# A Mamba-2 block with a mixture of experts behind it: other turns, engines and loads for the weights of the projection's first group

## The reference, cut to what matters

```
h = rmsnorm(hidden_states, ln1_w)              # 2048 x 512
zxbcdt = h @ in_proj_w                         # 512 x 2576
z, xb, Bc, Cc, dt = split(zxbcdt)              # 1024, 256, 256, 1024, 16 columns
xBC = silu(causal_depthwise_conv([xb, Bc, Cc]))  # 4 taps
dt = softplus(dt + dt_bias)                    # step sizes
y = ssd_chunked(...) ; y = rmsnorm(y * silu(z)) @ out_proj_w
```

## Time and profile before

| | |
|---|---|
| time, median of 3 runs | 1441.54 us |
| the profiled execution, its time | 1440.74 us |
| its span | 1439.0 us |
| mean granted clock of PE | 0.986 |
| PE busy | 1379.0 us (96%) |
| DVE busy | 956.3 us (66%) |
| ACT busy | 640.9 us (45%) |
| POOL busy | 479.8 us (33%) |
| PE's first matmul of the projection | at 16.92 us |
| first matmul of groups 1, 2, 3 | at 89.31, 154.65, 219.61 us |
| last instructions of PE in the projection | 28 short matmuls from 279.69 us |

### The profile page before, as it was taken

One profiled execution on the slowest core, in us unless ns is written; L12 is line 12 of the kernel. 1 busy time (PEld: TensorE's weight loads), 2 busy tenths in 40 slices (PEclk: granted clock), 3 DMA queues, 4 the chain that ended last, 5 costly groups with the idle time before them and its releaser, 6 DMA issues.

```text
span 1439.0 us, 20651 instructions
## 1 busy us (share of the span) xinstructions
PE 1379.0 (96%) x7252; PEld 1107.2 (77%) x7252; DVE 956.3 (66%) x1314; ACT 640.9 (45%) x1123; POOL 479.8 (33%) x455
## 2 busy tenths in 40 slices
PE   6899999989999998999999999999999889999998
PEld 4677777756666665788888888888887689999997
DVE  6879697789999997233333333333336779999997
ACT  4444454455555554311121112121111348888886
POOL 2612021247777775210101101011101027556563
PEclk9999999999999999999999999999999979999999
DMA  9122221833333221500001000002033933444331
GB/s 206 60 106 103 84 89 59 245 107 108 117 118 114 103 104 52 191 30 15 30 15 29 29 15 29 15 29 95 0 110 126 340 99 66 80 73 76 72 48 22
DMA packets 84359, 122.62 MB, mean 85 GB/s; under 512 B 28591, under 2 KB 44975, under 8 KB 84272
## 3 DMA queue, kind: packets, MB, share of 16 engines
q1 hardware_dynamic: 71488, 103.62, 21.9%
q0 software_dynamic: 8736, 16.79, 6.7%
q10 hardware_dynamic: 4048, 1.10, 0.3%
HBM read 81.37 MB, written 43.78 MB: 87 GB/s over the span
## 4 chain that ended last, share of the span: by engine, by line
PE 56%; DVE 2%; issue 1%; ACT 0%; DMA 0%; POOL 0%; DVEq 0%; ACTq 0%; POOLq 0%
PE fin_bank L1894 53%; PE fin_bank L2035 1%; PE fin_bank L2054 1%; DVE onehot L1803 0%; PE fin_bank L1962 0%; DMA xs<-xn_rows,idx 0%; PE fin_bank L1950 0%; DVE ff_w_lo L1695 0%; ACT gu_hi L1586 0%; DVE fi_bn L1730 0%; DVE gu_lo L1824 0%; ACT ff_w_hi L1564 0%; PE fin_bank L2027 0%; POOL out_dram L1518 0%; PE fin_bank L1960 0%
## 5 line engine op out<-in xcount | busy, mean ns | idle before, releaser
L1657 DVE TENSOR_TENSOR ff_prod<-ff_prod,fin_bank 128x512 f32<-128x512 f32 x64 | 44.0, 688 | 263.1 <-PE fin_bank L1894 263.1
L1894 PE MATMUL fin_bank<-ff_hT_hi,ff_w_hi 128*128 128x512 f32 x512 | 202.7, 396 | 3.2 <-DVE ff_w_lo L1665 3.2
L1894 PE MATMUL fin_bank<-ff_hT_hi,ff_w_lo 128*128 128x512 f32 x512 | 202.4, 395 | 0.0
L1894 PE MATMUL fin_bank<-ff_hT_lo,ff_w_hi 128*128 128x512 f32 x512 | 202.4, 395 | 0.0
L1448 POOL TENSOR_TENSOR ff_w_lo<-ff_stage,ff_w_hi 128x1024 fp32r<-128x1024 f32 (+1 forms) x24 | 56.5, 2355 | 411.1 <-ACT ff_w_hi L1554 406.3
L543 DVE SCALAR_TENSOR_TENSOR conv_acc<-raw,conv_w,conv_acc 128x512 f32<-128x512 f32 x144 | 115.7, 804 | 41.6 <-ACT raw L349 35.4
L648 PE MATMUL pj_bank<-hT_hi,w_in_hi 128*128 128x512 f32 x336 | 136.0, 405 | 6.5 <-POOL w_in_lo L296 4.0
L1539 ACT ACTIVATE ff_prod<-fin_bank 128x512 f32<-128x512 f32 x64 | 38.3, 598 | 231.5 <-PE fin_bank L1894 231.5
L648 PE MATMUL pj_bank<-hT_lo,w_in_hi 128*128 128x512 f32 x336 | 133.7, 398 | 0.0
L648 PE MATMUL pj_bank<-hT_hi,w_in_lo 128*128 128x512 f32 x336 | 132.8, 395 | 0.0
L1824 DVE TENSOR_TENSOR gu_lo<-wx,gu_hi 128x1408 fp32r<-128x1408 f32 (+1 forms) x79 | 124.9, 1620 | 1.8 <-ACT gu_hi L1586 1.8
(11 more groups left out here) (287 smaller groups left out, 3213.3 us busy)
## 6 DMA issues: line engine op xcount, KB each, us to landing
cv_rows<-cst SPq DMA_DIRECT2D x12, 1024.0 KB, 4.3
cv<-cv_rows SPq DMA_DIRECT2D x16, 768.0 KB, 4.3
zs_rows<-zst SPq DMA_DIRECT2D x8, 1024.0 KB, 6.5
zs<-zs_rows SPq DMA_DIRECT2D x16, 512.0 KB, 5.3
wx<-in_L_ffn_Wg_dram SPq DMA_DIRECT2D x8, 704.0 KB, 8.6
wx<-in_L_ffn_Wu_dram SPq DMA_DIRECT2D x8, 704.0 KB, 8.5
w_raw<-in_L_attn_in_proj_w_dram SPq DMA_DIRECT2D x32, 128.0 KB, 3.6
x<-_attn_hidden_states_dram SPq DMA_DIRECT2D x16, 256.0 KB, 5.4
```

Source lines behind the costliest of these rows:

```text
L1657: eng.tensor_tensor(prod[c][:, :], prod[c][:, :], up_ps[c][:, :], ALU.mult).then_inc(s["prod"], 1)
L1894: mm = eng.matmul(ps, w[a], x[b], start=first and i == 0, stop=last and i == 2)
```

## The change

1. **Order in group 0.** `first_products(0)` was dt, ch 0-6, then z and ch in turn, then z 5-7. It is now dt, ch 0-4, then z and ch in turn (z 0 at place 6, ch 8 at place 13, z 4 at place 14), then z 7.
2. **Loads.** C and z are no longer loaded in pairs of heads but as they lie in DRAM, by three DMAs: C's first half, all of z, C's second half. They go to places of their own (`c_raw`, `z_raw`), laid over buffers that are needed later (`zst`, `cst[1]`, `hT_hi1` and `hT_lo1`), and the pairing is done by the access pattern with which ACT and DVE read them (`by_pair`, `pairs`). The twelve small vectors are issued by SP, between C's first half and z.
3. **Low parts.** All by DVE. In ACT's and DVE's list the quarters follow each other as C, z, C, z ("czcz"). ACT makes two high parts at each of places 2 to 7; DVE makes two low parts at each of the places in the table `LOWS`.
4. **Turned rows.** `turned` stands at the start of places 16 to 19 on ACT and DVE, ahead of the work on that place's block.
5. **Step sizes.** For groups 1 to 3 the dt block uses weights `wdt` of 32 columns, 16 of high and 16 of low parts side by side: 8 matmuls. The two halves land in different partitions, are turned together, and DVE adds them (one more instruction of 128 x 64 in `dt_first`). `wdt` is filled by two small copies of DVE ahead of `made`.

```diff
     if g == 0:
-        order = [("dt", 0)] + conv[0:7]
-        rest = conv[7:12]
-        for i in range(5):
-            order += [z[i], rest[i]]
-        return order + z[5:8]
+        order = [("dt", 0)] + conv[0:5]
+        for i in range(7):
+            order += [z[i], conv[5 + i]]
+        return order + z[7:8]
...
+        LOWS = {2: KD, 3: KD + 2, 6: 2 * KD, 8: 2 * KD + 2, 10: 3 * KD, 12: 3 * KD + 2}
...
+        def by_pair(t, kk, a):
+
+            return t[:, kk, a * DI // 2:(a + 1) * DI // 2].rearrange("p (b j n) -> p j b n", b=2, j=HPG)
+
+        def pairs(t, kk, at):
+            return t[:, kk, at:at + DI // 2].rearrange("p (j b n) -> p j b n", j=HPG, b=2)
...
-            for a, (dst, src) in heads_raw(W_C, c0):
-                eng.dma_start(dst, src).then_inc(s[f"wc{a}_dma"], 16)
-            for a, (dst, src) in heads_raw(W_Z, 0):
-                eng.dma_start(dst, src).then_inc(s["wz_dma"], 16)
+            half = DI // 2
+            eng.dma_start(c_raw[0][:, :, :], wr[:, :, c0:c0 + half]).then_inc(s["wc0_dma"], 16)
+            small_vectors(eng)
+            eng.dma_start(z_raw[:, :, :], wr[:, :, 0:DI]).then_inc(s["wz_dma"], 16)
+            eng.dma_start(c_raw[1][:, :, :], wr[:, :, c0 + half:c0 + DI]).then_inc(s["wc1_dma"], 16)
```

POOL's part goes:

```diff
-                    if g == 0 and 4 <= n <= 7:
-                        for j in range(2):
-                            split_z((n - 4) // 2, 2 * (n - 4) % KD + j)
```

In the loops over the places, `turned` moves on ACT (and in the same way on DVE) from behind the place's work to ahead of it:

```diff
                 for n, (kind, i) in enumerate(ORDER[g]):
+                    if g + 1 < NGRP and AT_TURN <= n < AT_TURN + KD:
+                        turned(g + 1, n - AT_TURN)
                     if kind == "dt":
...
-                    if g + 1 < NGRP and AT_TURN <= n < AT_TURN + KD:
-                        turned(g + 1, n - AT_TURN)
```

DVE's low parts:

```diff
-                    if g == 0 and 1 <= n <= KD:
-                        split(2 * KD + n, n - 1, W_C + 512, W_C + 1024)
+                    if g == 0 and n in LOWS:
+                        for j in range(2):
+                            split_heads(LOWS[n] + j)
...
+            def split_heads(i):
+
+                kk, kind, a = i % KD, "czcz"[i // KD], i // (2 * KD)
+                eng.wait_ge(s["w_hi"], KD + i + 1)
+                at = (W_C if kind == "c" else W_Z) + a * 512
+                src = by_pair(c_raw[a], kk, 0) if kind == "c" else by_pair(z_raw, kk, a)
+                eng.tensor_tensor(pairs(w_lo, kk, at), src, pairs(w_hi, kk, at).bitcast(F32), ALU.subtract)\
+                   .then_inc(s["wx_lo" if kind == "c" else "wz_lo"], 1)
```

The dt block of groups 1 to 3 on PE, in `product`:

```diff
+                if g and kind == "dt":
+                    eng.wait_ge(s["made"], 1)
+                    for k in range(KD):
+                        if k < KD - 1:
+                            eng.matmul(ps[0:2 * HEADS, :], wdt[:, k, :], x[0][:, k, :], start=(k == 0), stop=False)
+                        eng.matmul(ps[0:HEADS, :], wdt[:, k, 0:HEADS], x[1][:, k, :], start=False, stop=False,
+                                   skip_group_check=True)
+                    eng.matmul(ps[0:2 * HEADS, :], wdt[:, KD - 1, :], x[0][:, KD - 1, :], start=False, stop=True)\
+                       .then_inc(s["block_ps"], 1)
+                    return
```

More of the change, by code:

```diff
@@ L96, in project @@
         lnq = [sb(f"lnq{i}", [P, 4, UPG]) for i in range(2)]
+        with nc.sbuf_tensor("z_raw", [P, KD, DI], F32) as z_raw:
+            pass
         hT_hi = [keep["hT0"][0], sb("hT_hi1", [P, KD, GR], F32R)]
@@ L103, in project @@
         ztnh = [sb(f"ztnh{i}", [P, GR]) for i in range(2)]
-        cst = [sb(f"cst{i}", [P, UPG, 4, P]) for i in range(2)]
+        cst = [sb("cst0", [P, UPG, 4, P])]
+        with nc.sbuf_tensor("c_raw1", [P, KD, DI // 2], F32) as c_raw1:
+            pass
+        cst.append(sb("cst1", [P, UPG, 4, P]))
+        with nc.sbuf_tensor("c_raw0", [P, KD, DI // 2], F32) as c_raw0:
+            pass
+        c_raw = [c_raw0, c_raw1]
         zst = [sb(f"zst{i}", [P, UPG, 4, P]) for i in range(2)]
-        dtT = sb("dtT", [HEADS, GR])
+        dtT = sb("dtT", [2 * HEADS, GR])
+        wdt = sb("wdt", [P, KD, 2 * HEADS], F32R)
         sp = sb("sp", [P, 7, UPG * HEADS])
@@ L162, in xin_ready, with small_vectors @@
             return (s[f"xin_dma{u}"], 16) if g == 0 else (xin_next[g % 2], 16 * (1 + g // 2))
-        def heads_raw(at, src):
-            for a in range(2):
-                for b in range(2):
-                    for k in range(KD):
-                        cols = slice(at + a * DI // 2, at + (a + 1) * DI // 2)
-                        yield a, (w_raw[:, k, cols].rearrange("p (j b n) -> p j b n", j=HPG, b=2)[:, :, b, :],
-                                  wr[:, k, src + (2 * a + b) * HPG * DST:src + (2 * a + b + 1) * HPG * DST]
-                                  .rearrange("p (j n) -> p j n", j=HPG))
+        def by_pair(t, kk, a):
+            return t[:, kk, a * DI // 2:(a + 1) * DI // 2].rearrange("p (b j n) -> p j b n", b=2, j=HPG)
+        def pairs(t, kk, at):
+            return t[:, kk, at:at + DI // 2].rearrange("p (j b n) -> p j b n", j=HPG, b=2)
+        def small_vectors(eng):
+            cw, cb = ins["L0_attn_conv_w"], ins["L0_attn_conv_b"]
+            nb = 2 * DXB // P
+            with nc.allow_non_contiguous_dma("small vectors"):
+                loads = [(a_neg[:, :], ins["L0_attn_A_log"].partition_broadcast(P)),
+                         (dt_bias[:, :], ins["L0_attn_dt_bias"].partition_broadcast(P)),
+                         (conv_w[:, 0:nb, :], cw[0:2 * DXB, :].rearrange("(k p) t -> p k t", p=P)),
+                         (conv_b[:, 0:nb], cb[0:2 * DXB].rearrange("(k p) -> p k", p=P))]
+                for a in range(2):
+                    for b in range(2):
+                        half, at, src = slice(b * HD, (b + 1) * HD), nb + HPG * a, 2 * DXB + (2 * a + b) * HPG * DST
+                        loads += [(conv_w[half, at:at + HPG, :],
+                                   cw[src:src + HPG * DST, :].rearrange("(j n) t -> n j t", j=HPG)),
+                                  (conv_b[half, at:at + HPG],
+                                   cb[src:src + HPG * DST].rearrange("(j n) -> n j", j=HPG))]
+                for dst, src in loads:
+                    eng.dma_start(dst, src).then_inc(s["v_dma"], 16)
         @block.sync
@@ L549, in silu_ch @@
                 eng.wait_ge(s["ch_tanh"], m + 1)
+                if ch % 4 == 0 and q == 1:
+                    eng.wait_ge(s["wx_lo"], 3 * KD)
                 if ch % 4 == 0 and q >= 2:
@@ L576, in _ @@
             for k in range(KD):
[L577 removed]
+                split_heads(k)
             def tables():
```

83 lines of the change are left out of this document (38 added, 45 removed).

## The result

The changed kernel takes 1430.72 us (median of 4 runs, 1429.10 to 1431.76), the kernel before 1440.84 us beside it (1439.84 to 1441.88): a ratio of 0.993, 95% interval 0.9918 to 0.9941. The forecast was 1432.0 in a range of 1428 to 1437.

A forecast was written before the change was run, and what follows sets the result against it. The prediction took PE's waits in the projection, with DVE behind them, as the bound. Gains of 3.4 + 2.8 + 1.9 + 1.2 = 9.3 us took 1440.74 to 1431.4, for a median 1432 us; range 1428 to 1437.

The forecast's parts named there:

- Group 0: Projection's first group: group 1 begins at 85.9 instead of 89.31 us, a gain of 3.4 us.
- The list of DVE: DVE's summed work in group 0 up to place 12, which z 4 waits for; it ends at 62.96 us.
- the wait for POOL's halo: Group 0, place 8: DVE waits 1.35 us for POOL's halo copy, which stands behind `norms`, before ch 6's taps.
- in front of z 4: Group 0, place 14: PE stands 5.0 us for DVE's low parts of place 12; the wait has moved, not gone.
- The low clock's cost: Group 0, behind PE's pause at z 4: a clock loss of 1.5 us, bounds 0 and 2.
- Step sizes: dt blocks of groups 1 to 3: 12 to 8 matmuls at 0.232 us each, a gain of 2.8 us.
- The change from 1 to 2: Group 2 begins at 152.7 instead of 154.65 us after a 1.5 us wait for the last turned part; gain 1.9.
- the one from 2 to 3: Group 3 begins at 218.35 instead of 219.61 us, with PE still standing 0.85 us for a turned part; gain 1.2.
- The start: Loads and first rows ahead of the projection: counted as 0, with bounds of 2 us later and 1 us earlier.
- z's load being late: Rival at the start: z lands after 29 us and holds ACT before ch 2's copy; 1434 to 1437 us, 12%.
- The rule of ring order: Start: one queue's descriptors go in order, so small vectors land behind C's first half, not before about 17.6 us.
- DVE keeps up: Rival in group 0: no wait at z 4 and no low clock; 6.6 us more gain, 1425.5 us, 7%.

The follow-up runs named there:

- Experiments 6: Changed kernel with POOL's norms in group 0 behind the halo copy of channel block 6 instead of before it; 1428.00 us.
- experiment 7: Changed kernel with group 0's statistics of the next rows moved to the end of place 12, their scaling and POOL's norms to place 13; 1426.01 us.
- experiment 2: Changed kernel with the dt block of groups 1 to 3 by twelve matmuls of 128 columns again, without DVE's extra addition; 1433.53 us.
- experiment 1: Changed kernel with only the twelve small vectors issued from ACT's queue at the start again; 1434.67 us.
- Experiment 4: Kernel before the change with one part alone: turned parts stand first at their places on ACT and DVE; 1436.63 us.
- the ten profiles: Profiles of the changed kernel and nine follow-up runs with the small vectors on SP; first projection matmul at 14.41 to 15.37 us in the nine.
- Experiment 9: Changed kernel with group 0's old block order, and low parts of C's second half at places 5 and 6; 1426.20 us.
- experiment 5: Changed kernel with z's eight low parts made by POOL, two each at places 2, 3, 6 and 7; 1429.16 us.

## Why the prediction was right, and where it was not

**Group 0.** The list of DVE was right nearly step by step: the wait for POOL's halo 1.46 (1.35), taps of 2.3, low parts of 0.61 in the new patterns, 4.97 us in front of z 4 (5.0). In front of z 0, where 0.3 us were forecast, PE does not wait. Experiments 6 and 7 show by what they take away that this list, and within it the halo and the work on the next rows, sets z 4's time. The gain was still 2.6 us and not 3.4: the group was 69.75 us long, by the prediction's steps 68.98 (16.92 to 85.9; its last sum gives 85.8). Of the 0.8 us between, 0.6 lie behind z 4, where the low clock is.

**The low clock's cost is not a fixed number.** Seven blocks and the turns behind z 4 took 23.52 us (60.75 to 84.27). In experiment 7, without such a pause there, they took 21.59 (79.79 less 56.73 and less the 1.47 at the turn). So the clock cost 1.9 where 1.5 was taken, inside the bounds of 0 and 2. But with the same pause it cost 1.1 in experiment 2 (61.16 to 83.83) and 2.3 in experiment 1 (65.23 to 89.15), which is outside them. The forecast of 1.5 lies among these; a single profile tells this term to about 0.6 us.

**Step sizes, group changes.** 2.8 us, shown by experiment 2. The change from 1 to 2 gave 1.9 as forecast, with 1.22 us at group 2's first matmul instead of 1.5; the one from 2 to 3 gave 1.0 instead of 1.2, with 0.95 at the third turn instead of 0.85. Experiment 4 shows both in the kernel before, with the same two waits. The mechanism (what stood behind taps now stands behind softplus, silu and taps once more) is the one that was forecast.

**The start was the step that failed.** The prediction took 0 with a bound of -1, because it looked for the price of the second queue only in DVE's waits between the rows (1.0 us). The first rows themselves also land 1.0 us earlier. These two are 2.0 of the 2.4 us; DVE's scaling of the rows, at 8.39 instead of 10.80, has all of it. Even the smallest start gain of the ten profiles, 1.5 us, is outside the bound. The worry on the other side, z's load being late, did not come true, but it was near: z was issued at 17.01 and landed 8.0 us later, at 25.0, and ACT began its first high part of z at 25.50, without a wait. The vectors' own time had little to spare too: experiment 1 shows 2.0 us in front of z 0 when they land at 23.5. The rule of ring order fits the trace in kind: the first vector, issued at 5.98 behind the large loads, took 8.0 us to land, and the last, issued at 16.36, took 2.4. But the time worked out by it, not before 17.6 us, was wrong: the first vector landed at 14.0 and C's first half (issued at 5.43, 9.3 us) at 14.7, both sooner than the rate of 303 GB/s gave. The last vector was bound by SP's issuing.

**What the sum hid.** The forecast of the total was right to 1.3 us, and part of that is luck: the profiled gain of 10.8 us has 2.4 us of the start that no term held, and lacks 0.8 of what was forecast for group 0 and 0.2 at the last group change. Nor does the total say anything of the order's own worth. The new order was counted as part of "group 0 gains 3.4", and no term asked what the old order would give with the new low parts. Experiment 9 shows that it would give 3.7 us more in that group and 4.5 us of time (with the low parts of C's second half moved to fit). So "C and z take turns" lost what other parts gained, and the rival "DVE keeps up" (1425.5) was close to reach: 1426.0 by moving the next rows' work (experiment 7), 1426.2 by the old order.

**Open.** Experiment 4's time fell by 3.5 us where its projection ended 4.6 earlier, which was not followed further; experiment 5's fell by 1.6 where it was 3.2, and the low clock seen for it is that of one profile. How issuing from two queues holds up the first rows was not taken apart, and neither was why one and the same pause costs 1.1 us in one run and 2.3 in another.
